# Scatters of the second batch's rows: each but the first waits for an up product of the first batch

## The reference

```
x = x + attention0(layernorm(x))        # 16 heads of 64, biases, softmax
x = x + experts0(layernorm(x))          # 8 experts, 128 -> 512 -> 128, each token to its best one
x = x + statespace1(layernorm(x))       # conv, selective scan over 1024 steps, 16 states
x = x + experts1(layernorm(x))          # 8 experts, 128 -> 256 -> 128, all of them, gated

# experts0, the part that the change is in:
logits = (x @ wg_red.T) @ wg_unit.T ;  idx, score = argmax, max of softmax(logits)
for e in range(8):
    h = gelu(x @ w1[e] + b1[e])
    out += (idx == e) * (h @ w2[e] + b2[e])
out *= score
```

## Time and profile before

| | us |
|---|---|
| median of 3 runs | 1102.87 |
| the profiled execution | 1107.8 |
| its span | 1106.5 |
| PE busy | 1055.6 (95%) |
| DVE busy | 887.2 (80%) |
| POOL busy | 766.9 (69%) |
| ACT busy | 629.7 (57%) |

### The profile page before, as it was taken

One profiled execution on the slowest core, in us unless ns is written; L12 is line 12 of the kernel. 1 busy time (PEld: TensorE's weight loads), 2 busy tenths in 40 slices (PEclk: granted clock), 3 DMA queues, 4 the chain that ended last, 5 costly groups with the idle time before them and its releaser, 6 DMA issues.

```text
span 1106.5 us, 18453 instructions
## 1 busy us (share of the span) xinstructions
PE 1055.6 (95%) x6696; PEld 651.6 (59%) x6696; DVE 887.2 (80%) x1272; ACT 629.7 (57%) x930; POOL 766.9 (69%) x400
## 2 busy tenths in 40 slices
PE   8999999999999999999999999779789997999998
PEld 4555655665656656666656657767344443446786
DVE  6878887887887877878977747236999999997987
ACT  5554655555555555534545545348885766657653
POOL 5788889787887897877999820230888899794200
PEclk9999999999999999999999999989899999999999
DMA  6010110010010010010011354473654443340000
GB/s 216 1 33 13 35 40 21 21 39 21 20 41 21 20 40 21 20 40 20 25 45 31 91 180 135 133 231 116 215 183 169 150 156 134 136 155 14 11 10 20
DMA packets 64867, 83.72 MB, mean 76 GB/s; under 512 B 25757, under 2 KB 43725, under 8 KB 64777
## 3 DMA queue, kind: packets, MB, share of 16 engines
q1 hardware_dynamic: 61768, 79.46, 22.7%
q0 software_dynamic: 1024, 2.10, 0.6%
q10 hardware_dynamic: 1984, 0.98, 0.3%
HBM read 76.09 MB, written 6.28 MB: 74 GB/s over the span
## 4 chain that ended last, share of the span: by engine, by line
PE 80%; issue 8%; DVE 5%; POOL 4%; ACT 1%; DMA 1%; another core or an unknown queue 0%; POOLq 0%; DVEq 0%; ACTq 0%
PE psum L695 21%; PE psum L651 16%; PE psum L681 6%; PE psum L669 4%; PE psum L986 4%; PE psum L1080 4%; PE psum L721 3%; PE psum L1063 3%; PE psum L780 3%; POOL hc L2340 3%; PE psum L736 3%; PE psum L844 2%; PE psum L855 2%; DVE psum L2011 2%; PE psum L760 2%
## 5 line engine op out<-in xcount | busy, mean ns | idle before, releaser
L2252 POOL TENSOR_TENSOR psums<-psums,prob 128x1024 f32<-128x1024 f32 x180 | 431.9, 2400 | 26.1 <-POOL psums L2252 0.5
L1694 DVE TENSOR_REDUCE mx<-psum 128x2 f32<-128x1024 f32 x256 | 301.2, 1217 | 92.9 <-PE psum L681 92.5
L1201 ACT ACTIVATE prob<-psum 128x1024 f32<-128x1024 f32 x202 | 206.1, 1027 | 55.6 <-PE psum L669 38.9
L695 PE MATMUL psum<-prob,V 128*64 128x512 f32 x1024 | 236.5, 597 | 0.0
L2340 POOL TENSOR_TENSOR hc<-hs,cc 128x1024 f32<-128x1024 f32 x64 | 151.5, 2368 | 19.7 <-DVE hs L2018 17.0
L2018 DVE TENSOR_TENSOR_SCAN hs<-dA,psum 128x1024 f32<-128x1024 f32 x64 | 146.3, 2286 | 2.2
L695 PEld LDWEIGHTS psum<-prob,V 128*64 128x64 f32 x1024 | 67.9, 137 | 115.1 <-issue 108.1
L986 PE MATMUL psum<-hc,ident 128*128 128x512 f32 x256 | 123.7, 606 | 2.8 <-DVE slot_rows_h L2026 1.5
L2252 POOL TENSOR_TENSOR psums<-prob 128x1024 f32<-128x1024 f32 x30 | 72.2, 2406 | 71.8 <-ACT prob L1201 71.1
L1220 ACT COPY oraw<-psum 128x512 f32<-128x512 f32 x32 | 18.8, 588 | 176.0 <-PE psum L695 176.0
L681 PE MATMUL psum<-k_hi,q_hi 64*128 64x512 f32 x512 | 107.9, 410 | 1.7 <-DVE mx L1694 1.3
(11 more groups left out here) (324 smaller groups left out, 1787.2 us busy)
## 6 DMA issues: line engine op xcount, KB each, us to landing
cc<-C_rows SPq DMA_DIRECT2D x64, 512.0 KB, 3.7
slot_rows_h<-guard_rows SPq DMA_DIRECT2D x56, 256.0 KB
kq_wts<-in_e_rows SPq DMA_DIRECT2D x14, 578.0 KB, 3.9
e_wts<-in_e_rows SPq DMA_DIRECT2D x10, 578.0 KB, 3.9
e_w<-in_e_rows SPq DMA_DIRECT2D x6, 578.0 KB, 5.8
slots_in<-e_zero SPq DMA_DIRECT2D x2, 960.0 KB, 7.1
inv<-sum_rows SPq DMA_DIRECT2D x120, 1.0 KB, 2.0
slots_out<-e_y SPq DMA_DIRECT2D x30, 64.0 KB, 1.8
```

What stands on the lines that cost most here:

```text
L695: ins = pe.matmul(A.O[HALF[s], :], A.V[pair % 2][:, j, s * DH:(s + 1) * DH], A.prob[unit(pair, c, j) % NPB][:, s * CH:(s + 1) * CH], start ...
L1201: act.activation(A.prob[n % NPB][:, :], slots.bank("score", pair, c, j).rearrange("p s n -> p (s n)"), ACT.Exp, scale=float(DH) ** -0.5).t ...
L1694: dve.tensor_reduce(K.A.mx[:, :, t, c], slots.bank("max", pair, t, c), AXX, ALU.max).then_inc(*slots.inc("max", pair, t, c))
L2252: pool.tensor_tensor(total[:, :], (K.A.prob[(n - 1) % NPB] if j == 1 else total)[:, :], K.A.prob[n % NPB][:, :], ALU.add).then_inc(*K.psum ...
```

## The change

Each scatter of the second batch but the first gets a wait ahead of it. With 8 tiles to a batch (`NT`) and 15 slots (`NSLOT`), t is 8 to 15 for the second batch. Tile 8 has no new wait; tiles 9 to 14 wait for `up` 9 to 14, and tile 15 for `up` 14 again. The first batch's tiles are 0 to 7 and stay as they were. No instruction is added, removed or moved on any engine but for the waits, which stand at these seven DMAs on POOL.

```diff
@@ pool_scatter
     if b == 0 and quarter == 0:
         pool.wait_ge(*K.ld["slots_zero"])
     for t in (b * NT + 2 * quarter, b * NT + 2 * quarter + 1):
+        if t > NT:
+            pool.wait_ge(*K.work.full.at("up", min(t, NSLOT - 1)))
         pool.indirect_dma_start(out=R.slots_in[b], ...
```

## The result

The change takes 1107.57 us, the median of its runs, against 1102.87 us for the kernel before, run beside it: a ratio of 1.0047 with a 95% interval of 1.0036 to 1.0059, thus 4.0 to 6.5 us slower. The forecast was 1100.5. Rival 1 had stood at 1106.9. The profiled execution of the changed kernel took 1107.5 us, its span is 1106.2. The profiled 1107.8 us of before lie above all 19 of its timed runs here (1098.07 to 1106.66); each later profile is one of its own kernel's timed runs. On which occasion the profile of before was taken is not on record.

What follows compares the result with a forecast made beforehand. It took PE, held back by late reports during POOL's runs of indirect DMAs, as the bound. Gathers and what follows come 2.4 us earlier: 1102.87 - 2.4 = 1100.5 us, own range 1099.3 to 1102.2, with slower rivals 1099.0 to 1107.2.

Steps and rivals of the forecast that it cites:

- Rival 1: Routed stage: timed runs have no stall, or POOL doesn't cause it; load waits until 713.8, slower by 4.0, 1106.9; chance 0.20.
- What bounds the kernel now: Routed stage: runs of indirect DMAs on POOL hold back PE's reports; DVE and ACT see finished products 5 to 6 us late.
- When the scatters go: POOL, second batch: scatters follow the ups from 697.9, the eighth at 711.7 instead of 706.89, 4.8 us later than before.
- The pitch of 1.78 us on PE: PE, second batch's slots: an up and the down behind it take 1.78 us where nothing waits.
- Rival 2: Second batch's scatters: one alone holds PE's report back, pitch 2.7 us; slower by 2.3, 1105.2; chance 0.14.
- When they have landed: Eighth scatter's data: landed 2.1 us after issue, at 713.8; a weight fetch in the way gives up to 715.5.
- What follows it: After ACT's load: gelu 14 at 714.8, down 14 3.3 us earlier, transposes 2.2 earlier, gathers 2.4 earlier.
- The low clock: PE after 4.7 us idle: clock 0.50, so down 14 takes 2.08 us instead of 1.16, 0.9 more.
- The gathers' stall: PE at the first batch's eight gathers: the stall stays as it was and ends 2.4 us earlier.
- The sum: Whole kernel: span 1106.5 less 2.4 is 1104.1, time 1102.87 less 2.4 is 1100.5; effect bounds 0.7 to 3.3.
- The rule of the Trainium skill: Second batch's scatters: by this rule the change can only lose, the load's data being ready 4.8 us later.

Runs made afterwards that it cites:

- B: Second measuring occasion, with its own runs of the kernel before, whose median there was 1107.75 us.
- C: Third measuring occasion, with its own runs of the kernel before, whose median there was 1108.25 us.
- E: Fifth measuring occasion, on the same chip as D; the kernel before had a median of 1108.09 us there.
- F: Sixth measuring occasion, with its own runs of the kernel before, whose median there was 1109.13 us.
- 1: Unchanged copy of the kernel before, profiled again on B: 1108.17 us, ratio 1.0012 to before.
- 13: Unchanged copy of the kernel before, profiled on E: 1110.09 us, ratio 1.0015 to before.
- 17: Unchanged copy of the kernel before, profiled on F: 1108.04 us, ratio 1.0000 to before.
- 2: Kernel before with one wait alone, the eighth scatter (tile 15) on up 14, on B: 1113.12 us, ratio 1.0052 to before.
- 8: Kernel before with ACT's first two loads of slot rows moved behind gelu 14, on C: 1107.55 us, ratio 1.0003 to before.
- 3: The change with its seven waits on earlier products, two scatters to an up, on B: 1106.48 us, ratio 0.9997 to before.
- 7: The change with both earlier gates (two scatters to an up) and earlier weight fetches, on C: 1107.45 us, ratio 0.9993 to before.
- 16: The change with early gates and ACT's loads behind gelu 14, same kernel as 9, on E: 1108.31 us, ratio 1.0001 to before.
- A: Occasion of the main result: the kernel before had a median of 1102.87 us there, the change 1107.57 us.
- D: Fourth measuring occasion, on the same chip as E; the kernel before had a median of 1103.02 us there.
- 9: The change with early gates (two scatters to an up) and ACT's loads behind gelu 14, on D: 1103.24 us, ratio 1.0006 to before.
- 5: The change itself, unaltered, measured again on C: 1110.53 us, ratio 1.0028 to before.
- 14: The change itself, unaltered, measured a third time, on E: 1110.95 us, ratio 1.0018 to before.
- kernel 6: The change with ACT's first two loads of slot rows moved behind gelu 14, on C: 1105.53 us, ratio 0.9971 to before.
- 15: The change with ACT's loads behind gelu 14, same as kernel 6, on E: 1106.43 us, ratio 0.9986 to before.
- 12: The change with ACT's loads behind gelu 14, same as kernel 6, on D: 1103.90 us, ratio 1.0011 to before.
- kernel 4: The change with the weight fetches for slots 16 and 17 issued earlier, behind slots 8 and 9, on B: 1108.77 us, ratio 1.0015 to before.
- kernel 11: The change with tiles 14 and 15 waiting for up 13 instead of up 14, on D: 1106.44 us, ratio 1.0034 to before.
- 18: The change with loads behind gelu 14 and the first batch's gathers set apart by waits, on F: 1106.87 us, ratio 0.9986 to before.

## Why the prediction was wrong

**What bounds the kernel now: right for the profile, wrong for the timed runs.** The stall is real; eight profiles on B, C, E and F repeat it at the scatters (1, 13 and 17, copies of before, and 2 and 8; 3, 7 and 16 with about half of it), and on the same occasions it is gone where the scatters are set apart. But the timed runs of A were free of it, as far as can be told: their median equals that of D, where none of four profiles has PE waiting over 1.4 us at scatters or gathers for what it had long reported. The step that failed is "I go by the profiled execution, span 1106.5 us in a time of 1107.8, 4.9 over the median of the runs, and carry the difference over to 1102.87". The profile stood 4.9 us above the median, and above every timed run of A, and I argued the gap away because two full stalls would be 9.8 us. The pairs of kernels say what they are worth: 9 and 16 differ by 5.1 us between occasions, before by 5.1 (D and E), the change by 3.0 and 3.4 (5 and 14 against A), kernel 6 by 1.6 and 2.5 (6 and 15 against 12). Adding up PE's waits overstated the stall by a factor of two; in kernel 16 the work behind the scatters' part of it caught up entirely.

**When the scatters go: right.** Kernel 14 opens like before, so its rows can be laid beside mine. Forecast 701.5, 703.3, ..., 711.7; measured on POOL

```profile
701.67 0.96 POOL L2265 DMA_INDIRECT slots_in<-xrows,posi  x1 [2.75 <-PE psum L844]
703.94 0.96 POOL L2265 DMA_INDIRECT slots_in<-xrows,posi  x1 [1.31 <-PE psum L844]
...
712.52 0.96 POOL L2265 DMA_INDIRECT slots_in<-xrows,posi  x1 [0.30 <-issue]
```

0.8 us late at the end, and in pairs rather than evenly. The pitch of 1.78 us on PE, no idle time there and the stall gone at the scatters were all as predicted, in the change's three profiles. Rival 2, that one scatter is enough for a late report, is out.

**When they have landed: the term that was mis-sized.** I took 2.1 us (bound 715.5 for the landing). It is 4.50 in kernel 14, 3.53 in 5, 4.64 in A, and 2.26 only beside little other traffic. The load goes out at 717.02, not 713.8, 3.2 us late of the forecast and 0.75 later than before's 716.27, so the gain of that step was none even with the stall:

```profile
717.02 0.94 ACTq L1555 DMA_DIRECT2D slot_rows_h<-slots_in  x2
718.08 1.14 ACT L1317 ACTIVATE slot_rows_h<-psum,e_wts 128x128 f32<-128x128 f32 x4 [8.36 <-issue]
```

The bound was too tight for the same reason as the value. It counted the fetch's bytes and left out the three or four slot stores and what passes between the last bytes and the release (1.1 us in kernel 4). Which of these makes a landing long isn't shown: kernels 12 and 15 are one kernel with 6.5 and 3.3 us. The nearest row that held a full landing was one I didn't use: the load's 5.81 us in the earlier trace rows.

**What follows it: right in form.** The rows are those of kernel 14 again. The low clock came as counted (down 14 takes 2.07 us):

```profile
719.27 2.07 PE L855 MATMUL psum<-e_wts,slot_rows_h 128*128 128x128 f32 x8 [8.05 <-ACT slot_rows_h L1317]
721.14 1.06 PE L831 MATMUL psum<-ident,slot_rows_h 128*128 128x128 f32 x4
```

The transposes start 0.96 us later than in before and the gathers (724.09) 0.95 later, where 2.2 and 2.4 earlier were forecast. The gathers' stall moved along, 4.33 us for 3.31, which varies from one execution to the next (3.27 to 5.08). In the profiles this makes the stage 3.1 us longer than before's (65.0 for 61.9). The timed runs near 1108 have 2.0 us (14) and 3.1 (5), with intervals from 0.3 to 3.5 and from 1.7 to 4.4, so that they confirm the direction more than the size.

**The sum.** Of the 7.1 us between 1100.5 and 1107.57, 3.2 are the landing. Then there was no stall to remove: the change loses 0.18 to 0.28% where before is stalled (0.18 being near what copies differ by) and 0.47% on A, and kernel 11, which acts like it, 0.34% on D. The difference of 0.19 to 0.29% is 2.1 to 3.2 us. The 0.7 to 1.8 us that are left are about what copies differ by and have no explanation here. Rival 1's 1106.9 came near with a working that was half right. It had the load wait from 709.8 to 713.8; in fact it goes out at about 717.0 (718.64 less the opening's 1.6), and an unhindered before could not have issued it before about 710.3 either (706.9 + 3.4, by the landings of kernels 3 and 7). That estimate gives over 6 us where the interval says 4.0 to 6.5, so some is caught up later. How much can't be told without a profile of before free of the stall. That the rival's number fell within 0.7 us of the result is in part luck. The rule of the Trainium skill that I weighed (DMA: Bandwidth & Descriptors, Rules for kernel authors), to issue a DMA early and wait for it late, was the better guide: kernel 6 keeps the late issue and restores the late wait, and beats the change by 0.57% and 0.32% on C and E.

What stays open: what in the chip delays PE's reports, and what makes an occasion have it. That the stall is absent from timed runs of before near 1103 is inferred from its time and from five profiles on A and D, all of other kernels, not seen in a profile of before.

## What to carry to other kernels

When the profiled execution lies above the timed runs by more than the effect you forecast, the pattern you mean to remove may be the difference itself; first look at a second profile, or make the forecast twice, with the pattern and without. The excess alone proves nothing: the profile of kernel 11 stands 3.0 us over its median without a stall of over 1.4 us. Before holding back a DMA, find the first instruction that waits for it and everything queued behind that on its engine: moving that wait behind work that doesn't need the data gave back all that the hold-back cost on C and E (0.57% for 0.28, 0.32% for 0.18). Take a landing from issue to the waiter's start, never to the last bytes moved.

## What the runs showed of the hardware

- Eight indirect DMAs in a row on POOL can delay what DVE and ACT see of PE, by 5.7 and 6.3 us in the earlier trace rows. Seven scatters and eight gathers did so on one occasion and not on another, with the same kernel on the same chip (9 and 16). With scatters 1.8 us apart on average, in pairs 1.3 us apart, none of the six profiles on stalled occasions that have them shows a wait of PE there (4, 5, 6, 14, 15, 18); runs of four and three 1.26 us apart leave 1.9 us of it.
- An indirect scatter of 64 KB released its waiter 2.26 us after its issue with little other traffic (DMA share 0.06 to 0.36), and 3.3 to 6.5 us after it where it was the last of the set and more moved beside it (in the changed kernel share 0.80 to 0.98 from 714 to 717), with a weight fetch or without.
- PE's clock fell to 0.50 for some 3 us near 10 us in seven of the 20 profiles, of either kernel, and not in the others: the first projection takes 1.94 us for 1.08 there, and 1.6 us later at the first scatter (699.45 for 697.90; 699.54 for 697.95 in two copies of before, 13 and 17).
